# Delta product of the second write as one stacked fp32r product, and inverse sums of the first write spread by stacked fp32r products

## The reference, cut to what matters

```
def rat_write(res, y, wod_w, wab_w, wab_b, du_w, du_b):
    o_d = y @ wod_w.T
    A_B = y @ wab_w.T + wab_b
    out = o_d[..., :H]                      # H = 512
    delta_low = o_d[..., H:]                # 8 columns
    ...
    delta = softplus(delta_low @ du_w.T + du_b)
    A_neg = -softplus(A_logit)
    A_bar = exp(delta * A_neg)
    B_bar = (A_bar - 1.0) / (A_neg - SSM_EPS) * B_proj
    B_bar_skip = delta * B_skip
    return hs * A_full + out * B_full       # A_full = [A_bar, 1], B_full = [B_bar, B_bar_skip]
```

## Time and profile before

| | us |
|---|---|
| median of 3 runs | 2239.14 (2226.57 to 2247.09) |
| the profiled execution | 2235.39 |
| its span, first to last instruction | 2233.3 |
| PE busy | 2109.5 (94%) |
| DVE busy | 1479.1 (66%) |
| POOL busy | 1185.9 (53%) |
| ACT busy | 1087.5 (49%) |
| mean granted TensorE clock | 0.971 |

### The profile page before, as it was taken

How to read it: one execution, slowest core, us unless ns; L and a number is a source line. 1 busy time by engine, 2 the same in 40 slices (tenths; PEclk the granted TensorE clock), 3 DMA queues, 4 the chain that set the end, 5 groups by cost and what they waited for, 6 DMA issues and landing times.

```text
span 2233.3 us, 34661 instructions
## 1 busy us (share of the span) xinstructions
PE 2109.5 (94%) x11176; PEld 1732.0 (78%) x11176; DVE 1479.1 (66%) x1950; ACT 1087.5 (49%) x1700; POOL 1185.9 (53%) x717
## 2 busy tenths in 40 slices
PE   6998889999998999799999999999889999999999
PEld 4777766666666888778888899999678877888887
DVE  6778766777765788644665527766877665757663
ACT  3445447888884677732221235666533222223231
POOL 0111137999997677600000047777567676666464
PEclk9999998999998899899999999999999999999999
DMA  5677862343324666567898747887998699897796
GB/s 189 208 241 246 261 194 82 98 106 97 100 68 127 243 217 216 189 197 241 295 330 275 250 159 288 303 298 292 333 347 296 217 316 312 284 303 257 257 326 203
DMA packets 259629, 516.93 MB, mean 231 GB/s; under 512 B 20979, under 2 KB 136691, under 8 KB 240965
## 3 DMA queue, kind: packets, MB, share of 16 engines
q1 hardware_dynamic: 259524, 515.60, 69.2%
HBM read 359.81 MB, written 155.45 MB: 231 GB/s over the span
## 4 chain that ended last, share of the span: by engine, by line
PE 50%; DVE 5%; DMA 4%; issue 3%; ACT 3%; POOL 2%; SPq 0%; DVEq 0%; POOLq 0%; ACTq 0%
PE s_m_psG L2342 8%; PE s_m_psU L2342 8%; PE s_psF L2938 7%; PE s_psF L2939 7%; PE s_psF L2940 7%; PE s_w_psA L1906 4%; PE s_w_psB L1906 4%; DMA s_f_xs<-xnT 2%; PE s_w_psR L1405 1%; PE s_w_psT L1938 1%; POOL s_f_xs L2894 1%; DMA s_f_xl<-xnT 1%; DVE s_w_ab L1674 1%; PE s_w_psT L1923 1%; DVE s_f_acc L2835 1%
## 5 line engine op out<-in xcount | busy, mean ns | idle before, releaser
L1052 POOL TENSOR_TENSOR s_a_pl<-s_a_pf,s_a_ph 128x1024 fp32r<-128x1024 f32 x128 | 301.8, 2391 | 22.2 <-ACT s_a_pf L1009 22.1
L2894 POOL TENSOR_TENSOR s_f_xs<-s_f_xl,s_f_xs 128x1024 f32<-128x1024 f32 x80 | 204.1, 2552 | 144.6 <-DMA s_f_xs<-xnT 144.4
L2078 POOL TENSOR_TENSOR s_w_yl<-s_w_y,s_w_yh 128x1024 fp32r<-128x1024 f32 x32 | 76.0, 2397 | 365.7 <-ACT s_w_yh L1986 365.7
L947 DVE TENSOR_REDUCE s_a_mx<-s_psS 128x1 f32<-128x512 f32 (+2 forms) x248 | 179.3, 754 | 98.1 <-PE s_psS L875 97.7
L2767 ACT ACTIVATE s_f_xh<-s_f_xs 128x1024 fp32r<-128x1024 f32 x80 | 84.9, 1061 | 287.5 <-POOL s_f_xs L2894 287.5
L2818 DVE TENSOR_TENSOR s_f_xl<-s_f_xs,s_f_xh 128x1024 fp32r<-128x1024 f32 x80 | 109.4, 1368 | 156.4 <-ACT s_f_xh L2767 156.4
L2938 PE MATMUL s_psF<-s_f_wh,s_f_xh 128*128 128x512 f32 x448 | 175.5, 392 | 9.0 <-DVE s_f_acc L2835 7.7
L448 POOL TENSOR_TENSOR s_q_qk<-s_q_ra,s_q_rb 128x1024 f32<-128x1024 f32 x16 | 37.7, 2358 | 272.7 <-DVE s_q_rb L691 272.7
L1006 ACT ACTIVATE s_a_ph<-s_psX 128x1024 fp32r<-128x1024 f32 (+1 forms) x160 | 150.6, 941 | 52.6 <-PE s_psX L903 48.8
L2939 PE MATMUL s_psF<-s_f_wl,s_f_xh 128*128 128x512 f32 x448 | 175.1, 391 | 0.0
L2940 PE MATMUL s_psF<-s_f_wh,s_f_xl 128*128 128x512 f32 x448 | 175.0, 391 | 0.0
(11 more groups left out here) (335 smaller groups left out, 6388.7 us busy)
## 6 DMA issues: line engine op xcount, KB each, us to landing
s_f_xl<-xnT SPq DMA_DIRECT2D x112, 512.0 KB, 5.5
s_f_xs<-xnT SPq DMA_DIRECT2D x80, 512.0 KB, 7.0
s_q_xt<-xT SPq DMA_DIRECT2D x16, 1024.0 KB, 7.5
s_q_xc<-xP SPq DMA_DIRECT2D x16, 1024.0 KB, 9.9
hsD<-s_q_hs SPq DMA_DIRECT2D x16, 1024.0 KB, 4.8
s_w_hin<-hsD SPq DMA_DIRECT2D x16, 1024.0 KB, 5.1
hs<-s_w_res SPq DMA_DIRECT2D x16, 1024.0 KB, 3.8
s_m_raw<-giT SPq DMA_DIRECT2D x32, 512.0 KB, 5.7
```

The costliest lines, as they stand in the source:

```text
L947: dve.tensor_reduce(mx[:, slot % 2, qi:qi + 1], psS[:, off:off + (qi + 1) * P], AX, ALU.max).then_inc(mx_ok, 1)
L1052: pool.tensor_tensor(pl[:, r, cols], pf[:, j - 1], ph[:, r, cols], ALU.subtract).then_inc(pl_ok, 1)
L2894: pool.tensor_tensor(xs[i % 3][:], xl[u % 4][:].bitcast(F32), xs[i % 3][:], ALU.add if product(u)[1][1][2] > 0 else ALU.subtract).then_inc ...
```

## The change

In the **second write** the delta product becomes one fp32r product. Its contraction grows from 9 to 96 rows: three groups of 32, 9 used in each and the rest zero. `zd` holds (high, low, high) of the nine columns, `du` holds (high, high, low). DVE makes `zd` for each tile with two operations at the start of its step, ahead of `update`: a copy that rounds (L2172, two groups at once) and a subtraction (L2174). `turn_small` transposes `zd` in place of `pa` and waits for both. For the last tile the two operations stand among the feed-forward's first preparations. `du` is prepared in the MLP (one memset, three small DMAs, two copies and a subtraction more).

In the **first write** `rr` and `pick` get 32 rows: the inverse sums twice, high part and negated low part, against the identity and its negative. `spread_sums` becomes four fp32r products and moves ahead of `turn_small`. DVE makes `pick` (L1229, L1232) during the last part of attention, and splits the sums of the first 1024 rows (L1222, L1224) after attention's last evacuation, those of the other 1024 in step 5 of the write. The load of the sums takes two DMAs in place of one for each half. Semaphores that the first write has done with are used again.

```diff
@@ second write @@
-        du = sb("w_du", [S0, H])
+        du = sb("w_du", [3 * LOW, H], F32R)
...
-        dlT = sb("w_dlT", [S0, P])
+        dlT = sb("w_dlT", [3 * LOW, P], F32R)
+        zd = sb("w_zd", [P, 3 * LOW])
...
             def turn_small(s):
-                pe.wait_ge(pa_ok, count(s - 2, 2, 1))
-                pe.wait_ge(one_ok, 3)
+                pe.wait_ge(z_ok, count(s - 2, 2, 2))
...
-                pe.transpose(psT[0][0:S0, 0:P], pa[:, s.off % 2, 0:S0], k["ident"][:]).then_inc(dl_mm, 1)
+                pe.transpose(psT[0][0:3 * LOW, 0:P], zd[:], k["ident"][:]).then_inc(dl_mm, 1)
...
+            def split_low(s, p):
+
+                dve.wait_ge(pa_ok, count(s - 2, 2, 1))
+                if (s - 3).exists():
+                    dve.wait_ge(dl_mm, count(s - 3, 1, 1))
+                cells = zd[:].rearrange("p (g j) -> p g j", j=LOW)
+                dve.tensor_copy(cells[:, 0:3:2, 0:S0].bitcast(F32R), spread(pa[:, p, 0:S0].unsqueeze(1), P, 2, S0)).then_inc(z_ok, 1)
+                dve.wait_ge(z_ok, count(s - 2, 2, 1))
+                dve.tensor_tensor(cells[:, 1, 0:S0].bitcast(F32R), pa[:, p, 0:S0], cells[:, 0, 0:S0], ALU.subtract).then_inc(z_ok, 1)
...
             def body(s, p, live):
+                if live(2) and live(1):
+                    split_low(s, p)
                 if live(3):
                     update(s, 1 - p)
@@ feed-forward, DVE @@
-        def vector_ahead(dve, i):
+        def vector_ahead(dve, i, split):
             if i == 0:
                 lo_x(dve, 0)
                 lo_x(dve, 1)
-                for n in range(HK):
+                lo_piece(dve, 0)
+                lo_piece(dve, 1)
+                split()
+                for n in range(2, HK):
                     lo_piece(dve, n)
@@ first write @@
+        def split_inverse(dve, b):
+            dve.wait_ge(rr_in, 32 * (b + 1))
+            dve.tensor_copy(rs[:, b], rr[:, b]).then_inc(rs_ok, 1)
+            dve.wait_ge(rs_ok, 2 * b + 1)
+            dve.scalar_tensor_tensor(rs[:, b], rr[:, b], second[0:2 * NH, :], rs[:, b], ALU.mult, ALU.subtract).then_inc(rs_ok, 1)
...
-                inv = rr[:].rearrange("h b t -> h (b t)")[:, ds(s.at(P), P)]
+                inv = rs[:].rearrange("h b t -> h (b t)")[:, ds(s.at(P), P)]
...
+                if live(0):
+                    spread_sums(s)
                 if live(1):
                     turn_small(s, q, live)
-                if live(0):
-                    spread_sums(s)
```

More of the change, by code:

```diff
@@ L46 @@
 NEG = -1e30
+LOW = 32
 EXP_LN_SET = 6
@@ L1092, in build_write1 @@
         spf = sb("w_spf", [P, KD * 2 * HD + HD])
-        pick = sb("w_pick", [NH, KH, P])
+        pick = sb("w_pick", [2 * NH, KH, P], F32R)
         pa = sb("w_pa", [P, 2, 1 + NW])
@@ L1098, in build_write1 @@
         bet = sb("w_bet", [P, 2 * KH])
+        second = sb("w_second", [P, 1])
         sb = shelf(nc, "s3_", zone["tables"], zone["XB"])
@@ L1159, in prepare_scalar @@
             act.activation(c64[:], flat64[:], ACT.Copy).then_inc(ready, 1)
-            act.activation(pick[:].rearrange("h g (n d) -> h (g n) d", d=HD),
-                           spread(k["ident"][0:NH, 0:NH].unsqueeze(2), NH, NH, HD), ACT.Copy).then_inc(ready, 1)
             for part, raw in enumerate((wraw0, wraw1)):
@@ L1192, in prepare_gpsimd @@
             pool.tensor_tensor(brow[64:P, :], braw[64:P, :], brow[64:P, :], ALU.subtract).then_inc(ready, 1)
-            pool.wait_ge(ready, 8)
+            pool.wait_ge(ready, 7)
         folded = "n (q j) -> (n q) j"
@@ L1214, in load_inverse, with prepare_tables @@
             sp.wait_ge(rec_out, 16 * (b + 1))
-            sp.dma_start(rr[:, b], io["oR"][b * NH:(b + 1) * NH]).then_inc(rr_in, 16)
+            for j in range(2):
+                sp.dma_start(rr[j * NH:(j + 1) * NH, b], io["oR"][b * NH:(b + 1) * NH]).then_inc(rr_in, 16)
+        def split_inverse(dve, b):
[3 more added lines that the diff above has]
+            dve.scalar_tensor_tensor(rs[:, b], rr[:, b], second[0:2 * NH, :], rs[:, b], ALU.mult, ALU.subtract).then_inc(rs_ok, 1)
+        def prepare_tables(dve):
+            ident = k["ident"]
+            dve.wait_ge(ready, 7)
+            dve.tensor_tensor(pick[:].rearrange("h g (n d) -> h (g n) d", d=HD),
+                              spread(ident[0:2 * NH, NH:2 * NH].unsqueeze(2), 2 * NH, NH, HD),
+                              spread(ident[0:2 * NH, 0:NH].unsqueeze(2), 2 * NH, NH, HD), ALU.subtract).then_inc(pick_ok, 1)
+            dve.tensor_reduce(second[0:2 * NH, :], ident[0:2 * NH, NH:2 * NH], AX, ALU.max).then_inc(pick_ok, 1)
+            dve.wait_ge(pick_ok, 2)
         o_in = [sem(f"o_in{p}") for p in range(2)]
@@ L1290, in vector_ahead @@
         def vector_ahead(dve, i):
+            if i == 0:
+                prepare_tables(dve)
             if i == 1:
                 invert_sums(dve, 0)
+            if i == 3:
+                split_inverse(dve, 0)
         def sync(sp, after):
@@ L1411, in tensor @@
             pe.wait_ge(w_lo, 2)
-            pe.wait_ge(ready, 8)
-            pe.wait_ge(rr_in, 16)
+            pe.wait_ge(ready, 7)
+            pe.wait_ge(pick_ok, 2)
+            pe.wait_ge(rs_ok, 2)
             def body(s, p, live):
@@ L1441, in body @@
                     read(s)
+                if s.reg is None and s.off == 5:
+                    pe.wait_ge(rs_ok, 4)
             steps(pe, TILES, LAST, 2, body, LAST + 2, after=after)
@@ L1694, in body @@
                     statistics(s)
+                if s.reg is None and s.off == 5:
+                    split_inverse(dve, 1)
                 if live(2):
@@ L1816, in sync_ahead @@
                 sp.dma_start(braw[:], io["bsm2"]).then_inc(small_in, 16)
-                sp.dma_start(du[:], io["du2"]).then_inc(small_in, 16)
+                sp.wait_ge(du_zero, 1)
+                for j in range(3):
+                    sp.dma_start(duraw[j * LOW:j * LOW + S0], io["du2"]).then_inc(du_in, 16)
             if i >= RW:
@@ L2047, in body @@
                         act.wait_ge(d_mm, count(s - 3, 1, 1))
-                    act.activation(dlT[:], psT[0][0:S0, 0:P], ACT.Copy).then_inc(dl_ok, 1)
+                    act.activation(dlT[:], psT[0][0:3 * LOW, 0:P], ACT.Copy).then_inc(dl_ok, 1)
                     if not live(1):
@@ L2180, in body @@
                     statistics(s, 1 - p)
-            steps(dve, TILES, LAST, 2, body, LAST + 1, after=after)
+            last = Step(None, TILES + 1, TILES)
+            steps(dve, TILES, LAST, 2, body, LAST + 1, after=lambda i: after(i, lambda: split_low(last, 1)))
         first = Step(None, 0, TILES)
@@ L2967, in build_rest @@
     spent = TAKEN[held:]
+    first = len(TAKEN)
     w1 = build_write1(nc, io, k, zone, qkv, att)
+    spent += [handle for handle in TAKEN[first:] if not any(handle is kept for kept in w1["kept"])]
     plane = build_plane(nc, io, k, zone)
@@ L3038, in _ @@
             mlp["vector"](dve, w2["vector_ahead"])
-            w2["vector"](dve, lambda i: ffn["vector_ahead"](dve, i), lambda i: ffn["vector_amid"](dve, i))
+            w2["vector"](dve, lambda i, split: ffn["vector_ahead"](dve, i, split), lambda i: ffn["vector_amid"](dve, i))
             ffn["vector"](dve)
```

28 lines of the change are left out of this document (21 added, 7 removed).

## The result

The changed kernel is slower: 2285 us against 2237 (medians), ratio 1.023 with a 95% interval of 1.018 to 1.028. One of its four executions was a slow one of 4056 us and is left out of that median and ratio; with it the median is 2290. The profiled execution took 2284.8, span 2282.8, 49.5 longer than the span of before.

| stage begins at PE | before | after | added in the stage before it |
|---|---|---|---|
| attention | 319.0 | 321.8 | 2.8 (the change touches nothing there; the experiments' traces have 318.6 to 324.1) |
| attention's last product | 686.0 | 694.4 | 5.6 |
| first spread | 686.2 | 697.4 | 2.8 |
| MLP | 945.6 | 956.9 | 0.1 |
| second write, psB | 1301.7 | 1313.0 | 0 |

What follows compares the result with a forecast made beforehand. PE was taken to bound the second write, with an equally long chain. Terms 29 + 2.2 - 1 + 2.4 + 0.7 + 0.5 + 6 = +39.8 on 2235.4 gave 2275, plus 3.75 for the median: 2279, range 2235 to 2303.

Steps and rivals of the forecast that it cites:

- case A: Second write: copy and subtraction both held by GpSimd, mean 20.15 us a tile against 17.72, +29 us; chance 0.55.
- What bounds the kernel: Second write's steady part: PE busy 238.56 of 240 us, with an equally long chain through ACT, DVE and POOL.
- the chain round from delta product to L2109: Second write: delta product, ACT, reciprocal, L2109, back to the delta product; 17.74 us against 17.69 measured, without slack.
- The split: Second write: copy and subtraction ahead of `turn_small`, held by GpSimd, start it about 2.8 us behind L2109; +2.43 a tile.
- The last tile: Into the feed-forward: the split stands behind four operations, so the first feed-forward product comes 2.2 us later.
- The clock: Whole kernel: PE gaps of over 2 us may bring half-clock stretches; +6 us taken.
- The start: First write: the first spread must wait for the split of the sums and begins about 689.2, +2.4 us.
- The gain of the spreads: First write: fp32r spreads save 0.5 us 16 times, mostly turned into waiting; -1 us, ends 0 and -8.
- `pick`: DVE among attention's last tiles, two SBUF inputs beside a busy POOL: +0.7 us, ends 0 and +2.4.
- Rival C: Second write: the split passes POOL unheld, 0.3 to 0.5 us a tile gained; 2238 us, not slower; chance 0.2.
- The loop of VectorE and GpSimd: Second write: DVE and POOL's own loop of 17.2 us, other parity about 17.3 to 17.5, limits PE's saving.
- Rival B: Second write: only the subtraction is held, mean 17.7 to 17.9 us a tile; 2245 us; chance 0.2.

Runs made afterwards that it cites:

- e4: The changed kernel, with the split's rounding copy writing all three groups of nine columns in place of two: 2282 us.
- e6: The changed kernel, with the split's copy written as a multiplication by 1.0 with a scalar: 2287 us.
- e3: The changed kernel, with ScalarE copying the nine columns into a PSUM bank, where the split's two VectorE operations read them: 2244 us, ratio 1.004 to before.
- e5: The changed kernel, with the split's rounding copy on ScalarE and the subtraction left on VectorE: 2248 us, ratio 1.008 to the kernel before.
- e8: The first write's part alone on the kernel before, with pick made after attention's last evacuation: 2246.6 us, ratio 1.008.
- e1: The second write's part of the change alone, the first write as in the kernel before: 2273 us, ratio 1.016.
- e7: The second write's part alone, split read from PSUM, last tile's split moved between the feed-forward's first two lo_x operations: 2225.6 us, ratio 0.998 to before.
- e2: The first write's part of the change alone, the second write as in the kernel before: 2253 us, ratio 1.008.

## Why the prediction was right

It said 2279 with 2235 to 2303, by case A; 2285 was measured. On the profiled execution it forecast +39.8 us, and the stages that the change can touch have +46.7 (49.5 less the 2.8 ahead of attention). The mechanism is that of case A. That the sum is so near is luck in part: two of its terms are wrong in opposite directions. Step by step:

- **What bounds the kernel** was right, and the chain round from delta product to L2109 was the thing to add to.
- **The split.** Both operations are held, and GpSimd's half goes between them, as in case A. `turn_small` came 2.5 us behind L2147 where 2.8 was said. The products came 19.4 and 21.5 us apart, mean 20.5, where 19.8 and 20.5, mean 20.15, were said; but 1.4 of the 21.5 is half clock, and without it the two are 19.4 and 20.1, mean 19.8. So the hold was priced some 0.4 us a tile too high. The reason given for the copy, its double pace, was not tested as such; e4 and e6 show that the hold needs neither an even count nor a copy. The Trainium skill ("VectorE: DVE Perf Modes", What auto-detection actually checks) gives a one-source operation its two-port pace when source and destination are in SBUF and their outer counts are both even or equal; e4's are equal, three and three, and its copy is held (2.17 us median), which agrees with that rule and doesn't test it.
- **The last tile**: +2.2 said, 2.2 found.
- **The clock**: +6 was taken for the whole; in the second write alone half-clock stretches cost some 13 us (eight steps of 1.4 to 2.7). Second write, tail and clock together: 37.2 said (29 + 2.2 + 6), 38.6 found. Taken apart it is 29 said for the hold and about 23 found, 6 said for the clock and 13 found. The errors cancel.
- **The first write.** The start was right (2.4 said, 2.8 found). The gain of the spreads is nil in the changed kernel's trace where 1 was said; in those of e3, e4, e5 and e8 the same stage is 3.2 us shorter than before, and what makes the difference wasn't tried. **The mis-sized term is `pick`**: 0.7 said with 2.4 as the upper end, 5.6 found. I priced it by its own length and let it wait for one GpSimd operation. A row of attention's end that I did not read has four of GpSimd's subtractions back to back, 9.4 us together; with such a row it could have been priced. These 4.9 us are most of the 6.9 that the forecast is short of. The traces of the experiments with `pick` at the same place have 5.6 to 8.1 us more in attention, that of e1, without it, 1.7.
- **Rival C**, made by e3 and e7, was priced about rightly: 0.3 to 0.5 us a tile was said to come, 0.53 came (17.13 against 17.66). The loop of VectorE and GpSimd, taken at 17.2 and 17.3 to 17.5, has a mean of 17.16 in e3. PE is ahead of it only for seven intervals, at 16.9. **Rival B**, made by e5: 17.45 us a tile where 17.7 to 17.9 was said.
- **A row that was not used.** No copy ran beside GpSimd in the kernel before, but single-input reciprocals did, and they were not held (`invert_sums`, L1207, 0.94 us). The case for "not held" was stronger than the prediction has it; that the copy was held all the same, only the run could show.

## What to carry to other kernels

A small VectorE copy, multiplication or two-input operation with all operands in SBUF isn't small beside a busy GpSimd: price it at the rest of the GpSimd operation under way, and at the next one too if it depends on another such operation. Let it read from PSUM (e3), or put it on ScalarE (e5), before the chain that PE waits for is made to pass through it. And a long row of GpSimd operations can hold an unrelated table preparation for all of its length: such work goes where GpSimd rests. Last, compare the granted clock of the runs, and not only their times: in e2 and e8 it goes with some 10 us of the loss, which no row of a hold explains.

## What the runs showed of the hardware that was not expected

- Some single-input VectorE operations from SBUF to SBUF are held too: copies of 2 x 9 and of 3 x 9 elements and a multiplication by a scalar, all 0.16 us at the shortest and 2.16 to 2.17 in the median here. Reciprocal and statistics are not (0.94, 0.44 and 0.68 us beside GpSimd). Reading the same nine columns from PSUM, the copy takes 0.18 at most.
- A held operation got in behind one GpSimd operation in the second write (e5), but `pick` was held over five in a row (10.02 us in two kernels, 0.67 behind them). What tells the two apart was not tried. In both places GpSimd's next operation follows without a gap.
- The lower clock follows some of PE's gaps and not others of the same length: in the changed kernel's steady part those of 2.93 us (0.61 for a product of 0.30) and not those of 2.33, in e4's those of 2.37 and not those of 2.93.
